# Moving six membrane comparisons from the head of one pass to the end of the pass before

## The reference, cut to what matters

```python
x = _layernorm(x + mamba(x))          # selective scan, 512 inner channels, 16 states
x = _layernorm(x + slot_attention(x, ctx))   # 3 rounds of attention and a GRU
# feed-forward with spiking neurons:
h = jnp.square(jax.nn.relu(x @ W_fc.T)); y = h @ W_proj.T
def step(mem, _):
    reset = spike_fn(mem - THRESHOLD)
    mem_new = BETA * mem + y - reset * THRESHOLD
    return (mem_new, spike_fn(mem_new - THRESHOLD))
spks = scan(step, zeros, length=5)
x = _layernorm(x + sum(spks) / 5)
```

## Time and profile before

| | |
|---|---|
| time, median of 3 runs | 1903.42 us (1899.98 to 1903.66) |
| the profiled execution | 1908.13 us |
| its span, first to last instruction | 1906.3 us |
| busy: VectorE, TensorE, ScalarE, GpSimd | 80%, 75%, 49%, 42% of the span |
| mean granted TensorE clock | 0.84 |

### The profile page before, as it was taken

The page is one execution under the profiler, slowest core; times in us unless marked ns, Lnnn a source line. Parts: engine busy times, 40 slices in busy tenths (PEclk is TensorE's granted clock), DMA queues, the critical chain, the costliest instruction groups (busy, mean ns, idle before and its releaser), DMA issues. The chain is left out here.

```text
span 1906.3 us, 15651 instructions
## 1 busy us (share of the span) xinstructions
PE 1431.9 (75%) x5136; PEld 789.3 (41%) x5136; DVE 1516.7 (80%) x1606; ACT 937.5 (49%) x1481; POOL 793.6 (42%) x411
## 2 busy tenths in 40 slices
PE   5556676776788679976788679886788769876965
PEld 2345233343345235453355335453355334452433
DVE  3987699967898799969998699968999699963242
ACT  4432654435653655636553645626563555633522
POOL 0665165514554155523554156523555055530000
PEclk9555878786899879997899979997899979897987
DMA  5632342206221343205231343205231243200000
GB/s 179 234 122 78 123 143 101 88 24 211 94 105 45 124 143 111 89 24 199 100 109 54 101 146 119 99 22 190 99 110 66 74 160 132 99 11 0 11 1 22
DMA packets 64760, 188.86 MB, mean 99 GB/s; under 512 B 6224, under 2 KB 22480, under 8 KB 64720
## 3 DMA queue, kind: packets, MB, share of 16 engines
q1 hardware_dynamic: 64720, 188.37, 28.7%
HBM read 183.62 MB, written 4.72 MB: 99 GB/s over the span
## 5 line engine op out<-in xcount | busy, mean ns | idle before, releaser
L428 POOL TENSOR_TENSOR reg_a<-reg_a,cb 128x1024 f32<-128x1024 f32 x256 | 612.1, 2391 | 500.5 <-DVE reg_a L1070 499.5
L1070 DVE TENSOR_TENSOR_SCAN reg_a<-reg_a,pb 128x1024 f32<-128x1024 f32 x256 | 584.2, 2282 | 19.7 <-ACT reg_a L855 6.9
L624 PE MATMUL py<-ident,reg_a 128*128 128x128 f32 x2048 | 328.3, 317 | 101.5 <-POOL reg_a L428 101.5
L855 ACT ACTIVATE reg_a<-dt,neg_a 128x511 f32<-128x511 f32 x512 | 336.3, 710 | 101.4 <-DVE reg_a L1070 101.4
L624 PEld LDWEIGHTS py<-ident,reg_a 128*128 128x128 f32 x2048 | 278.3, 164 | 225.0 <-POOL reg_a L428 130.9
L1061 DVE TENSOR_TENSOR pb<-bb,pb 128x1024 f32<-128x1024 f32 x256 | 314.5, 1228 | 25.3 <-DVE reg_a L1070 0.5
L528 PE MATMUL px<-hT,whh 128*128 128x512 f32 x384 | 204.3, 658 | 0.0
L513 PE MATMUL px<-hT,gT 128*64 128x512 f32 x96 | 65.0, 815 | 100.9 <-ACT xs L743 100.9
L602 PE MATMUL pc<-x2T,w_fc 128*128 128x512 f32 x224 | 123.6, 680 | 20.1 <-DVE reg_y L1087 12.3
L761 ACT ACTIVATE xs<-px,half_b 128x512 f32<-128x512 f32 x96 | 66.1, 688 | 143.1 <-PE px L532 142.9
L532 PE MATMUL px<-an,vw 64*128 64x512 f32 x192 | 120.3, 709 | 16.2 <-DVE an L974 16.1
(11 more groups left out here) (162 smaller groups left out, 1975.9 us busy)
## 6 DMA issues: line engine op xcount, KB each, us to landing
bb<-bc_rows SPq DMA_DIRECT2D x256, 512.0 KB, 3.6
cb<-bc_rows SPq DMA_DIRECT2D x64, 512.0 KB, 5.9
xin<-x_in SPq DMA_DIRECT2D x9, 512.0 KB, 3.5
xs<-x_in SPq DMA_DIRECT2D x8, 512.0 KB, 3.5
x_out<-reg_m SPq DMA_DIRECT2D x8, 512.0 KB, 3.4
w_in<-w_inT_in SPq DMA_DIRECT2D x1, 1024.0 KB, 6.8
w_fc<-w_fcT_in SPq DMA_DIRECT2D x1, 1024.0 KB, 10.9
w_pr<-w_prT_in SPq DMA_DIRECT2D x1, 1024.0 KB, 13.1
```

The lines of the kernel that those rows point to most:

```text
L428: pool.tensor_tensor(h[:, g % HR], h[:, g % HR], cb[:, 2 * q:2 * q + 2], ALU.mult).then_inc(s["hc_done"], 1)
L624: mm = pe.matmul(py[:, cols_], h[:, g % HR, j, cols_], ident[:], is_transpose=True, start=(q == 0 and j == 0 and i2 == 0), stop=(q == PAIR ...
L855: ins = act.activation(d_a[:, g % 2, j, 1:], dt[:, c, 1:], ACT.Exp, scale=neg_a[:, c * NS + n + j:c * NS + n + j + 1])
L1070: dve.tensor_tensor_scan(h2[:, g % HR], d_a2[:, g % 2], pb[:, 0:2, :].rearrange("p a t -> p (a t)"), 0.0, ALU.mult, ALU.add).then_inc(s["s ...
```

## The change

The six `spike` steps become steps of ffn: they run in the pass that computes `y_sb`, one pass earlier for the same batch. Their positions are "end" (n=0 and 1), "post" (n=2 and 3) and "leave" (n=4 and 5), a new position on VectorE behind `norm_apply("post")` and ahead of the meeting. Only VectorE takes the step, so no other engine's order changes. Two waits on `out_res` go. Two are added: n=0 waits for the last sum of `y_sb`, and n=5 for `x2_old` of its own pass. The steps run in passes 2 to 9 in place of 3 to 10.

```diff
-        for position, n in zip(("x", "x", "dt", "dt", "dt", "dt"), range(SPIKE_OPS)):
+        for position, n in zip(("end", "end", "post", "post", "leave", "leave"), range(SPIKE_OPS)):
             place(position, ("spike", n))
...
-        SPIKE_STEPS = ("spike", "out_stats", "out_norm")
-        FFN_STEPS = ("up", "down", "keep_x2")
+        SPIKE_STEPS = ("out_stats", "out_norm")
+        FFN_STEPS = ("up", "down", "keep_x2", "spike")
...
                 elif step == "keep_x2":
-                    if spikes:
-                        act.wait_ge(s["out_res"], 1)
                     act.activation(x2_old[:], x2[:], ACT.Copy).then_inc(s["x2_kept"], 1)
...
                 elif step == "out_stats":
-                    dve.wait_ge(s["out_res"], 1)
                     norm_stats("out", memv)
...
                 if n:
                     dve.wait_ge(s["spike"], n)
+                if n == STEPS:
+                    dve.wait_ge(s["x2_kept"], 1)
                 if n == 0:
+                    dve.wait_ge(s["unit_read"], reads_before(1, "down", TT - 1) + 1)
                     ins = dve.tensor_scalar(cnt, y_sb, SPIKE_AT[0], None, ALU.is_gt)
...
                 filler("post")
                 if mamba:
                     norm_apply("post", xres, x1)
+                filler("leave")
                 meet(dve, i + 2)
```

## The result

The changed kernel takes 1909.0 us (median of 17 runs, 1907.27 to 1914.11), the kernel before 1904.0 (17 runs, 1899.98 to 1910.13). The ratio is 1.0028, with an interval of 1.0017 to 1.0039: slower by 5 us, where +6.7 was forecast. The size came out close, but three terms of the sum were off and partly cancel.

A forecast was written before the change was run, and what follows sets the result against it. VectorE was busiest (80%), but ScalarE set the head's end and VectorE-TensorE exchange the pass end. Late post norms +9.7 and tail -3.0 gave +6.7 us, on the 1903.42 median 1910.1; range 1903 to 1915.5.

The forecast's parts named there:

- The head's removal at nothing: Head of passes with mamba: six VectorE comparisons leaving gain nothing, since ScalarE's step-size parts set the head's end.
- The pair at "end" at nothing: Between L1087 and the next norm: n=0 and 1 fit VectorE's idle stretch; at most 0.2 us in one pass, taken as nothing.
- the 0.6 us of slip: Pass end: GpSimd's gate L432 can slip by 0.6 us, covered by TensorE still busy with L584.
- The pair at "leave" at nothing: Behind the post norm: n=4 and 5 take 2.5 us and cost nothing, with 3.5 us of cover before ScalarE ends.
- n=3 would find GpSimd in possession: At "post": n=3 waits for GpSimd's power L385, so the norm starts 1.90 us late; chance 0.42.
- the undisturbed rival: At "post": the short power does not exclude VectorE, norm 1.21 us late, 0.93 per pass, total 1906.0 us; chance 0.20.
- the cover: Between the post norm's end and transposes L682: TensorE absorbs 0 to 0.55 us of the norm's delay, 0.28 taken.
- The tail at -3.0: Passes 8 to 9: statistics start 3.17 us earlier, up to 0.4 may be lost at the third up projection; -3.0 taken.
- TensorE's clock at no change: Heads and L584 over the passes: the sum took no change in TensorE's clock; better or worse had chance 0.09 each.
- heads of passes 3 and 5 turn slow: Clock-worse rival in the heads: fast heads become slow, adding 3.4 us, 1913.5 us and above; chance 0.09.
- a change of TensorE's stretches by more than 2 us: Sign that the prediction is wrong: TensorE's stretches change by more than 2 us in sum.
- The range's lower end, 1903: Whole kernel: the undisturbed case (1906.0) with 0.28 us of cover per pass on its low side.

The follow-up runs named there:

- the tail alone: Kernel before, comparisons still at the head in passes 2 to 7, but passes 8 and 9 do their own at their end: 1898.3 us, ratio 0.9963.
- eight small instructions: Changed kernel with eight small VectorE instructions (128 x 2 numbers into a pad) ahead of position "post" in passes with mamba and ffn; one run, 1907.4 us.
- the matched pause: Kernel with four comparisons at "leave", given seven bn_stats and one more small VectorE instruction at "post", no comparisons there: 1901.3 us, ratio 0.9982.

## Why the prediction was right, and where it was not

- The head's removal at nothing: right. L1051's idle time went from 2.42 to 4.58 in pass 3 and ScalarE still ends it.
- The pair at "end" at nothing: right, with the taking of turns as worked out. The kernel with this pair and four at "leave" is level with the one that has the gain of the tail alone (1897.7 and 1898.3). That n=0 would hold L432 up was within the 0.6 us of slip that was allowed for it.
- The pair at "leave" at nothing: right, and it holds for four (VectorE ends 1.41 us ahead of ScalarE). It ends with six.
- "n=3 would find GpSimd in possession": this step failed. The exclusion seen between long operations was carried over to a power of 4 numbers. The norm came 1.18 late and not 1.90, which is the undisturbed rival's 1.21. With the cover, 0.44 where 0.28 was taken, the shift is 0.74 per pass and not 1.62: 4.4 us in place of 9.7. The rule that the prediction took from the Trainium skill ("SBUF — State Buffer", section "Who interferes with whom"), by which the two engines exclude each other for a whole instruction, fits L432 and n=1, and L385 held up by n=2 (1.91). It does not fit the short power's side: with eight small instructions n=2 starts 0.43 us into it and is not held up.
- The tail at -3.0: its mechanism was right and measured -3.19. Its size was off by what TensorE gains behind it, 2.7, where a loss of up to 0.4 was expected. Tail alone: -6.1.
- TensorE's clock at no change: this was priced as a rival (heads of passes 3 and 5 turn slow, +3.4), and that happened, +3.2, in every profile of this placement. The prediction named a change of TensorE's stretches by more than 2 us as a sign that it is wrong, and this one came.
- The range's lower end, 1903, lies 1.3 under what its own terms give (1906.0 - 6 x 0.28 = 1904.3). Nothing hangs on it.

So the direct terms measured 4.4 - 5.9 = -1.5, and the kernel is 5.0 slower. Of the 6.5 between, the heads give 3.2, and the slots, read against the tail alone, another 2.2, both stretches in which TensorE's granted clock is lower. The last us is not placed: the two profiles of the kernel before can't show it, since their executions lay 4 to 6 us above their kernel's median. That the forecast of 1910.1 came so near is luck in part: 5.3 too much at "post", 2.9 too little gain in the tail, and 6.5 that the sum did not have, most of it with the clock.

What stays open is why TensorE's clock falls so in the changed kernel. It is not the late norm as such: the matched pause did not bring it. Nor does it need a held-up L385: with eight small instructions the power lasts 1.09, and all five heads are slow and the execution took 1907.4; with one comparison at "post" the power is held up to 1.91, and the execution took 1897.7 (one run each). The kernel with the matched pause still differs in having no comparisons at "post", in two more at "leave", and by 0.05 us of length per pass, and the runs don't tell these apart.

## What to carry to other kernels

Put work that nobody waits for behind the last thing that others wait for, not into a gap ahead of it: the gap at "post" was 1.12 us and the work 2.5, while behind the norm 6.3 us stood free (four comparisons in 4.9, and VectorE still 1.41 ahead). Weigh the passes of the pipeline's tail by themselves; here the tail gave 5.9 us, more than the late norm of six full passes cost by itself (4.4). And where TensorE changes between two clocks, differences of some microseconds need many runs: one profile of a kernel can lie 10 us off its median (the one with six at "leave": 1897.2 against 1907.6).

## What the runs showed of the hardware

- A GpSimd power of 128 by 4 numbers, 1.01 us, is held up by a VectorE operation with two SBUF inputs (1.91), but did not hold one up that began 0.43 us into it: that comparison took its undisturbed time. A GpSimd multiply of 128 by 512 does (n=1 2.17 in place of 1.22).
- A VectorE comparison with one SBUF input (n=0, 128 by 1024, float32 in, bfloat16 out, 0.69 us) holds such a multiply up as well: 1.65 in place of 1.27.
- A two-input VectorE operation that comes 0.03 us after the start of GpSimd's record still goes first (L385 2.12).
- The time of the same 24 matmuls moves between 5.35 and 7.2 us with the granted clock (1.00 in a window over a group of 5.35, 0.81 over one of 6.57), and which passes are slow differs between executions of one program. The heads of passes 3 to 7 were slow in 30 of 30 with two comparisons at "post", in 16 of 25 with none.
